# The bias of the edge product: an ACT copy into PSUM in place of an opening bf16 matmul

## The reference

```python
Qh = (x @ Wq.T + bq).reshape(n, H, D)      # H = 4 heads of D = 16
Kh = (x @ Wk.T + bk).reshape(n, H, D)
Vh = (x @ Wv.T + bv).reshape(n, H, D)
Ee = (edge_attr @ We.T + be).reshape(-1, H, D)
score = (Kh[src] * Qh[dst] * (1.0 / np.sqrt(D)) * Ee).sum(-1)
score = jnp.exp(jnp.clip(score, -5.0, 5.0))
msg = Vh[src] * score[..., None]
wV = jax.ops.segment_sum(msg, dst, num_segments=n)
x = _layernorm(x + wV.reshape(n, H * D), axis=-1)
```

## Time and profile before

| | us |
|---|---|
| median of 3 runs (1716.1 to 1716.64) | 1716.46 |
| the profiled execution's own time | 1715.64 |
| its span, first to last instruction | 1713.8 |
| PE busy | 1649.7 (96%) |
| PE weight loads (they overlap PE) | 1479.4 (86%) |
| DVE busy | 1318.6 (77%) |
| POOL busy | 1263.1 (74%) |
| ACT busy | 960.6 (56%) |

### The profile page before, as it was taken

The page is one execution under the profiler, slowest core; times in us unless marked ns, Lnnn a source line. Parts: engine busy times, 40 slices in busy tenths (PEclk is TensorE's granted clock), DMA queues, the critical chain, the costliest instruction groups (busy, mean ns, idle before and its releaser), DMA issues. The chain is left out here.

```text
span 1713.8 us, 47297 instructions
## 1 busy us (share of the span) xinstructions
PE 1649.7 (96%) x13047; PEld 1479.4 (86%) x13047; DVE 1318.6 (77%) x2198; ACT 960.6 (56%) x2864; POOL 1263.1 (74%) x1348
## 2 busy tenths in 40 slices
PE   7399999999999999999999999999999999999994
PEld 7298888888888888888888988888888888888884
DVE  6377878778778778778778778778778787787786
ACT  5355555555555556556556556556555555555554
POOL 4677777777777777777777777777777777777774
PEclk8699999999999999999999999999999999999997
DMA  7455554555554555555555555455445555545441
GB/s 240 126 149 132 144 134 131 145 133 132 144 133 133 143 132 135 140 135 135 138 135 137 133 138 139 133 137 138 134 131 145 134 131 144 133 132 145 132 124 62
DMA packets 198830, 234.44 MB, mean 137 GB/s; under 512 B 96742, under 2 KB 123180, under 8 KB 198684
## 3 DMA queue, kind: packets, MB, share of 16 engines
q1 hardware_dynamic: 156732, 147.96, 30.0%
q0 software_dynamic: 42080, 86.26, 20.9%
HBM read 226.67 MB, written 7.38 MB: 137 GB/s over the span
## 5 line engine op out<-in xcount | busy, mean ns | idle before, releaser
L260 POOL DMA_INDIRECT kv<-kv_table,idx x1315 | 1246.1, 948 | 416.5 <-issue 388.1
L654 PE MATMUL xg_bank<-x_hi,src_onehot 128*128 128x448 f32 x2079 | 786.4, 378 | 6.1 <-DVE src_onehot L786 6.1
L655 PE MATMUL xg_bank<-x_lo,src_onehot 128*128 128x448 f32 x2079 | 759.9, 365 | 0.0
L725 ACT ACTIVATE distance<-iota_w,dst_neg 128x64 f32<-128x64 f32 x1612 | 428.4, 339 | 0.0
L654 PEld LDWEIGHTS xg_bank<-x_hi,src_onehot 128*128 128x128 f32 x2079 | 391.8, 188 | 34.6 <-DVE src_onehot L786 6.3
L655 PEld LDWEIGHTS xg_bank<-x_lo,src_onehot 128*128 128x128 f32 x2079 | 392.3, 189 | 27.3
L751 ACT COPY xg_t_sb<-turn_bank 64x256 f32<-64x256 f32 x198 | 61.9, 313 | 616.9 <-PE turn_bank L665 612.1
L798 DVE SCALAR_TENSOR_TENSOR x_sel<-iota_v,src_block,xg_bank 128x448 f32<-128x448 f32 x297 | 202.0, 680 | 248.5 <-PE xg_bank L655 240.7
L786 DVE TENSOR_TENSOR src_onehot<-r_row,xg_bank 128x896 fp32r<-128x896 f32 x297 | 320.0, 1078 | 24.8 <-DMA r_row<-r_table 24.8
L643 PE MATMUL sum_ps<-onehot,msg 128*64 128x64 f32 x3224 | 224.4, 223 | 8.6 <-DVE msg L843 8.6
L643 PEld LDWEIGHTS sum_ps<-onehot,msg 128*64 128x64 f32 x3224 | 208.9, 138 | 17.2 <-DVE msg L843 9.4
(11 more groups left out here) (116 smaller groups left out, 957.8 us busy)
## 6 DMA issues: line engine op xcount, KB each, us to landing
attr_sb<-attr SPq DMA_DIRECT2D x201, 256.0 KB
dst_row<-dst_rows SPq DMA_DIRECT2D x402, 128.0 KB
kv<-kv_table,idx POOLq DMA_INDIRECT x1315
r_row<-r_table SPq DMA_DIRECT2D x99, 128.0 KB
q_win<-q_table SPq DMA_DIRECT2D x404, 24.0 KB
r_row<-r_table SPq DMA_DIRECT2D x99, 64.0 KB
idx<-src_tab SPq DMA_DIRECT2D x206, 4.0 KB, 4.1
kv_table<-kv_stage SPq DMA_DIRECT2D x7, 448.0 KB, 3.8
```

Source lines behind the costliest of these rows:

```text
L260: pool.indirect_dma_start(out=kv[:, slot, t, :], out_offset=None, in_=kv_table, in_offset=bass.IndirectOffsetOnAxis(ap=idx[:, slot, t:t + ...
L654: pe.matmul(xg, src_onehot[:, parity, u, :], x_hi[:, u, :], start=(u == 0), stop=False)
L655: mm = pe.matmul(xg, src_onehot[:, parity, u, :], x_lo[:, u, :], start=False, stop=(u == U - 1))
L725: made = act.activation(distance[:, t, :], iota_w[:, :], ACT.Square, bias=dst_neg[:, ds(g, 1), t:t + 1].rearrange("p o t -> p (o t)"))
```

## The change

ACT copies the bias straight into the PSUM bank, as fp32, and the four fp32 matmuls then accumulate onto what ACT wrote. The bias matmul L617 is gone, and with it `be_sb` and its preparation on POOL (L311, L327 to L340). `be_f`, the bias broadcast over 128 partitions, stays in memory for the whole kernel. A new helper `seed_edges(g, slot)` holds the ACT copy. It waits until DVE has read the bank's former contents (`kqe_made`), a wait that PE had before. PE now waits for the copy (`ee_seeded`). In `step(g)` ACT runs `seed_edges(g+2)` after the copy L758 of group g+1 and ahead of the second four squares. At the end of the setup's matmuls PE runs two matmuls of zeros into the two banks, once, which puts the banks into the state in which later matmuls accumulate.

```diff
-                if not (isinstance(g, int) and g < 2):
-                    pe.wait_ge(kqe_made, g - 1)
+                pe.wait_ge(ee_seeded, g + 1)
                 ee = bank(ee_ps[slot % 2], n * P)
-
-                pe.matmul(ee, ones[:, :], be_sb[:, 0:2 * n, :].rearrange("p t f -> p (t f)"),
-                          start=True, stop=False)
                 for k in range(n):
                     mm = pe.matmul(ee[:, k * P:(k + 1) * P], attr_sb[:, slot, k * P:(k + 1) * P],
-                                   we_sb[:, :], start=False, stop=(k == n - 1))
+                                   we_sb[:, :], start=False, stop=True, skip_group_check=True)
                 mm.then_inc(ee_made, 1)
...
+            def seed_edges(g, slot):
+
+                if not (isinstance(g, int) and g < 2):
+                    act.wait_ge(kqe_made, g - 1)
+                act.copy(ee_ps[slot % 2][:, :, :], be_f[:, :].unsqueeze(1).to_broadcast([P, T, F]))\
+                   .then_inc(ee_seeded, 1)
...
                     act.copy(kv[:, (j + 1) % SLOTS, T - turned:T, :], turn_bank[:, 2:2 + turned, :])\
                        .then_inc(pe_kv_made, 1)
                 if ahead:
+                    seed_edges(g + 2, slot2)
                     square_distances(g + 2, T // 2, T)
                     make_onehot(g + 2, slot2)
 
+            act.wait_ge(be_loaded, 16)
             for g in range(2):
+                seed_edges(g, g)
                 make_onehot_t(g, 0, g)
...
+        pe.wait_ge(kv_staged[0], CHUNKS)
+        pe.wait_ge(kv_staged[1], CHUNKS)
+        pe.wait_ge(consts_zeroed, 3)
+        for i in range(2):
+            pe.matmul(bank(ee_ps[i], 512), ones[:, :], q_win[:, :, :, :, :].rearrange("p a b c d -> p (a b c d)")[:, 0:512],
+                      start=True, stop=True).then_inc(ee_opened, 1)
+        pe.wait_ge(ee_opened, 2)
```

More of the change, by code:

```diff
@@ L92, in gnn_kernel @@
         zero_exp = sb("zero_exp", [P, 1], F32)
-        be_sb = sb("be_sb", [P, T, F], BF16)
+        be_f = sb("be_f", [P, F], F32)
         we_sb = sb("we_sb", [P, 2 * F], F32)
@@ L105, in gnn_kernel @@
         q_rest = sb("q_rest", [P, 2, CH, F], F32, first)
-        be_f = sb("be_f", [P, F], F32, first)
-        be_rest = sb("be_rest", [P, F], F32, first)
-        be_parts = sb("be_parts", [P, 3, F], BF16, first)
         dst_i = sb("dst_i", [P, G, T], I32, first)
@@ L164, in gnn_kernel @@
         be_loaded = sem("be_loaded")
-        be_step = sem("be_step")
         ones_set = [sem("ones_set_dve"), sem("ones_set_pool")]
@@ L170, in gnn_kernel @@
         ident_set = sem("ident_set")
+        ee_opened = sem("ee_opened")
         iota_set = sem("iota_set")
@@ L211, in gnn_kernel @@
         onehot_made = sem("onehot_made")
+        ee_seeded = sem("ee_seeded")
         ee_made = sem("ee_made")
@@ L233, in gnn_kernel @@
         pass_sems = range(attr_loaded[0].num, window_moved.num + 1)
-        assert len(pass_sems) == 6 * SLOTS + 26
+        assert len(pass_sems) == 6 * SLOTS + 27
         def pairs_of(g):
@@ L287, in _ @@
                                  kv_stage[:, c * CH:(c + 1) * CH, :]).then_inc(kv_stored, 16)
-                sp.wait_ge(consts_zeroed, 4)
+                sp.wait_ge(consts_zeroed, 3)
                 sp.dma_start(we_sb[0:F, 0:F], We_t).then_inc(we_loaded, 16)
@@ L310, in _ @@
                 pool.memset(we_sb[:, :], 0.0).then_inc(consts_zeroed, 1)
-                pool.memset(be_sb[:, :, :], 0.0).then_inc(consts_zeroed, 1)
                 pool.memset(q_win[:, :, :, :, :], 0.0).then_inc(consts_zeroed, 1)
@@ L325, in _ @@
                 pool.wait_ge(iota_set, 5)
[L327 to L340, removed]
                 pool.wait_ge(idx_first, 16 * SLOTS)
```

## The result

| | before | after |
|---|---|---|
| median us (4 runs each) | 1716.55 | 1787.70 |
| lowest to highest | 1716.1 to 1718.19 | 1786.28 to 1788.92 |
| the profiled execution's own time | 1715.64 | 1787.89 |
| its span | 1713.8 | 1786.0 |

The ratio is 1.0412, with a 95% interval of 1.0394 to 1.043: 71 us slower. The forecast was 95 us slower, 1811, with a range from 1790 to 1832. In their first runs the six kernels of the experiments met conditions under which the kernel before itself took 2754 to 2761 us, with PE pausing inside unbroken groups and mean granted clocks of 0.78 to 0.83; these runs are told apart from the others.

The account below looks back on a forecast made before the run. PE was taken as the bound, never waiting in the steady part, with POOL full as well. Two-tile copies cost +100 us and one-tile copies save 5, so +95 us on 1716.46 gives 1811.5; range 1790 to 1832.

Parts of the forecast that it names:

- PE sets the pace, POOL is full too: Steady part: PE busy for 300.00 of 300.00 us; POOL's 241 gathers with their issue time make 301 us.
- Place A: Two-tile copies: the bias copy queues behind L758 and PE's edge product waits; 1.01 us each, 99 times, 100 us.
- Place B: One-tile copies: the second gather lies between, so no wait; saves 0.05 us each, 5 us in all.
- a sum of 76 us: Variant with the edge product's weight load staying hidden behind the gather: one-tile copies save 24 us, total +76 us.
- What costs nothing: ACT's extra 0.5 us before the exponential, the start, POOL's shorter setup, the last groups (under 1 us): not counted.
- the shortest ladder: Low end for Place A: 0.27 + 0.585 + 0.05 against 0.93, so 0.99 us a time, 98 us.
- The signs of being wrong in size: In the changed profile, L729 or the first load behind it standing elsewhere than forecast.
- The longer ladder: Place A's copy starts only after L758 fully ends, with a wake-up of 0.20; 1835 to 1846 us; chance 0.09.
- The clock: Granted clock falls in PE's new gaps; some +160 us on top, about 1970 us; chance 0.02.
- The copy in time: ACT reaches the bias copy before PE needs it at Place A too; 1694 to 1712 us; chance 0.04.

Follow-up runs that it names:

- the control: Kernel before the change, with one of POOL's 13 gathers of each pair of groups left out from group 4 on; 1716.6 us, ratio 0.9997.
- the early seed: Changed kernel with ACT's bias copy moved directly behind the exponential of the same step; 1715.0 us, ratio 0.9993 to the kernel before.
- Place A alone: Changed kernel with only the odd groups seeded by ACT, the even ones keeping the bias matmul; 1811.1 us, ratio 1.0544 to the kernel before.
- the wide transposition: Changed kernel with the weights of transposition L651 padded with zeros from 64 to 128 columns; 1787.7 us, ratio 1.0414 to the kernel before.

## Why the prediction was wrong in size

- **PE sets the pace, POOL is full too.** Right, both ways: the control kept its time with a gather less, and the early seed won nothing with all of them. How exactly the two limits met, no row of the prediction showed.
- **Place A, 1.01 us.** Right: 1.00. The terms were 0.27 (0.27), 0.60 (0.59), 0.06 (0.05) and 1.15 (1.16) for the product from a standing start. Place A alone measured 93 us where its count gives 98, and the wait for the messages gives 5 back.
- **Place B, "I take 0.05 (L665 is the nearest row)".** This is the step that failed. It measured 0.22 us, 22 us in place of 5, and that is 17 of the 24 us. The prediction let the load open 0.30 us behind the gather and gave the product 1.15 us from there, as after a standstill; the product opened at 0.21 with its load already under way and took 1.05. The row chosen was another fp32 group behind L655 that waits, but with 64 columns of weights; the product has 128, as L655 has. The prediction had the Trainium skill's rule (TensorE: Matmul & The Clock Gate, "Step-by-step: what each phase is for": the queue pulls weight loads ahead of matmuls in flight) beside it, with a sum of 76 us, and set it aside on the strength of that row. The trace of after agrees with the rule at place B: the load starts at 812.02, with the gather's last matmul. L665's load is the exception, and the wide transposition shows what makes it one.
- **What costs nothing.** The sum of 95 - 17 - 5 = 73 us leaves nothing for the exponential, the start and POOL's setup, as forecast. The 5 are a wait of 0.05 us a pair that was overlooked. The row was in the prediction, read as a wake-up time. It was both.
- **The range.** Its low end was built from the full saving at place B and the shortest ladder, 1790. The truth lay at the full saving, and the hidden wait was in no bound, so the time fell out at the low end. Against the 73 us of the corrected sum the spans of the two profiled executions differ by 72.2 us and the medians by 71. The signs of being wrong in size looked at L729 and the load behind it, both at place A, where all was right; none looked at place B.
- **The rivals.** The longer ladder did not come, since the copies overlap as before. The clock stayed at 1.00 through pauses of 1.1 us in the steady windows. The copy in time was not this kernel's case; put in time by hand it gives 1715.0, above the 1694 to 1712 that was priced, because POOL's 22.3 us of waiting were one of 6.2 us at the start and 53 of 0.3 us, which is only its usual gap between gathers. There was nothing of it to give back.

## What to carry to other kernels

Work that is moved to an idle engine costs whatever its place in that engine's queue costs, not its duration. Here 0.6 us of ACT with 6 us of idle time in every pair (603.4 us in 98 pairs) cost PE 1.0 us, because the copy was queued behind one that waited for PE's own last instruction; a few lines earlier PE waits for it nowhere. When a cost is taken from the nearest row, match the shape of the operands before the kind of neighbour, and where a rule and one row disagree, look for a second row before you drop either. And before a saving is counted, look at how close the next limits are: an instruction that starts just a wake-up (0.06 us) behind another engine's end was waiting for it.

## What the runs showed of the hardware

- ACT wrote 128 x 512 fp32 values from SBUF into PSUM in 0.59 to 0.60 us (595 to 598 ns in 198 of the 202 records of the changed kernel), which lies among the 586 to 638 ns that the seven copies L387 of the same size from PSUM into SBUF took one by one in the kernel before (the row is the mean of four of them, 620): no run shows a gain clear of that spread.
- PE hides an fp32 weight load of 128 columns under a gather matmul of 448 columns (load and gather matmul both at 812.02), also where the group waits for semaphores that are already there. It doesn't hide it where the weights go from 128 to 64 columns: the group then opens 0.1 us later (0.30 in place of 0.21 us behind the gather) and shows its load. Padding only moved this (1787.7 us with it and without).
- PE stood still for 1.1 us in every 17, and the granted clock stayed at 1.00 (2.4 GHz) in the window from 100 to 400 us.
- POOL's indirect gathers of 128 rows started 1.249 us apart wherever nothing held them, in the kernel before and with the early seed alike.
